# Cross-attention kernel: the second tile's scores moved from the second softmax phase to the main loop's begin, the third tile's into the second tile

## What is computed

```
hs     = mha(x @ Wq, enc @ Wk, enc @ Wv)            # 2048 queries x 150 keys, the main loop
ca_q1  = einsum('btc,th->bch', ca, Wq_ca)[:, idx]   # 384 different rows, spread over 2048
ca_hs1 = mha(ca_q1, x, x)                           # softmax over 2048: the two phases
ca_hs2 = mha(ca_hs1 @ Wq, ca @ Wk_ca, ca @ Wv_ca)   # 4 tokens: the small p
out    = (hs + ca_hs2) @ Wout + b_out + x
```

## Time and profile before

| | |
|---|---|
| median of 3 runs | 1533.33 us |
| the profiled execution, its own time | 1535.76 us |
| its span, first to last instruction | 1534.0 us |
| mean granted TensorE clock | 0.998 |
| TensorE matmuls busy | 98% of the span |
| VectorE, ScalarE busy | 51%, 41% |

### The profile page before, as it was taken

The page is one execution under the profiler, slowest core; times in us unless marked ns, Lnnn a source line. Parts: engine busy times, 40 slices in busy tenths (PEclk is TensorE's granted clock), DMA queues, the critical chain, the costliest instruction groups (busy, mean ns, idle before and its releaser), DMA issues.

```text
span 1534.0 us, 24564 instructions
## 1 busy us (share of the span) xinstructions
PE 1499.9 (98%) x10310; PEld 1246.0 (81%) x10310; DVE 789.5 (51%) x1596; ACT 622.5 (41%) x1311; POOL 2.8 (0%) x12
## 2 busy tenths in 40 slices
PE   7999999999999999999999999999999999999998
PEld 5764799999975489999987549999998745999998
DVE  6785435344478363444448726435345873453533
ACT  2438633333244852332332584323233377333322
POOL 0000000000000000000000000000000000000000
PEclk9999999999999999999999999999999999999999
DMA  6640011120252001140045100213004410021101
GB/s 237 225 156 1 7 57 66 57 110 27 104 192 95 1 20 52 57 157 18 27 149 176 57 1 20 90 37 148 9 35 165 172 37 2 19 95 57 61 18 44
DMA packets 46680, 117.28 MB, mean 76 GB/s; under 512 B 3661, under 2 KB 5317, under 8 KB 45019
## 3 DMA queue, kind: packets, MB, share of 16 engines
q1 hardware_dynamic: 37036, 93.91, 17.6%
q10 hardware_dynamic: 9535, 21.80, 3.7%
HBM read 77.33 MB, written 39.17 MB: 76 GB/s over the span
## 4 chain that ended last, share of the span: by engine, by line
PE 91%; DVE 4%; ACT 2%; issue 1%; DMA 1%; SPq 0%; ACTq 0%
PE ps_w L511 47%; PE ps_s L511 18%; PE ps_t L511 16%; PE ps_t L521 6%; PE ps_w L521 3%; DVE unit_max L1329 2%; ACT work L1133 1%; PE ps_s L521 1%; ACT ot L1047 0%; DMA xc<-in_L_xattn_Wv_ca_dram 0%; DMA xc<-in_x_dram 0%; DVE ca_mat L1345 0%; DVE ot L1441 0%; ACT ot L1116 0%; DVE xt_l L1355 0%
## 5 line engine op out<-in xcount | busy, mean ns | idle before, releaser
L511 PE MATMUL ps_w<-wo_h,ot 128*128 128x320 f32 x1280 | 310.4, 314 | 0.6 <-DVE ot L1441 0.6
L1329 DVE TENSOR_REDUCE unit_max<-ps_s 128x1 f32<-128x512 f32 x384 | 240.6, 683 | 54.6 <-PE ps_s L511 53.6
L1103 ACT ACTIVATE work<-ps_s,neg_max 128x150 f32<-128x150 f32 x512 | 152.1, 402 | 223.4 <-DVE neg_max L1387 223.4
L511 PEld LDWEIGHTS ps_w<-wo_h,ot 128*128 128x128 f32 x1280 | 220.2, 188 | 0.9 <-DVE ot L1441 0.9
L511 PE MATMUL ps_w<-wo_l,ot 128*128 128x320 f32 x640 | 197.4, 308 | 0.0
L511 PEld LDWEIGHTS ps_w<-v_all,work 120*128 120x128 f32 x1280 | 170.3, 190 | 3.1 <-issue 2.5
L511 PE MATMUL ps_w<-v_all,work 120*128 120x162 f32 (+1 forms) x1280 | 171.3, 288 | 0.0
L1383 DVE TENSOR_REDUCE neg_max<-ps_s 128x6 f32<-128x900 f32 x64 | 70.0, 1094 | 165.2 <-PE ps_s L511 165.2
L511 PE MATMUL ps_s<-keys_h,qt_h 128*128 128x300 f32 (+1 forms) x448 | 140.0, 312 | 0.0
L511 PE MATMUL ps_s<-keys_h,qt_l 128*128 128x300 f32 (+1 forms) x448 | 131.5, 293 | 0.0
L511 PE MATMUL ps_s<-keys_l,qt_h 128*128 128x300 f32 (+1 forms) x448 | 131.1, 293 | 0.0
(11 more groups left out here) (171 smaller groups left out, 2352.3 us busy)
## 6 DMA issues: line engine op xcount, KB each, us to landing
xc<-in_x_dram SPq DMA_DIRECT2D x32, 1280.0 KB, 6.4
out_dram<-work ACTq DMA_DIRECT2D x64, 320.0 KB, 2.2
xt_all<-work SPq DMA_DIRECT2D x60, 256.0 KB, 2.2
xt_l<-xt_all SPq DMA_DIRECT2D x12, 1280.0 KB, 5.6
y_all<-in_L_xattn_Wk_dram SPq DMA_DIRECT2D x4, 960.0 KB
y_all<-in_L_xattn_Wv_dram SPq DMA_DIRECT2D x4, 960.0 KB
pick<-pick_all SPq DMA_DIRECT2D x16, 194.0 KB
xc<-in_L_xattn_Wq_dram SPq DMA_DIRECT2D x1, 1600.0 KB, 10.7
```

What stands on the lines that cost most here:

```text
L511: return nc.tensor.matmul(out, lhs, rhs, start=start, stop=stop, skip_group_check=True)
L1103: return nc.scalar.activation(probs[:, h * KEYS:(h + 1) * KEYS], ps_s[:, bank, c * KEYS:(c + 1) * KEYS], exp, bias=neg_max[:, s % 2, h:h + ...
L1329: v.tensor_reduce(unit_max[:, a, n, q:q + 1], bank, AX_X, ALU.max).then_inc(max_free, 1)
```

## The change

`RUNS_IN` loses its entries for tile 1, so that phase 1 holds only tile 0's last runs. In the main loop TensorE computes `tile_scores(s + 1)` at every tile but the last, ahead of `values(s)`: tile 1's scores come in tile 0, and tile 2's come in tile 1, behind `project(0, 0)`. The split runs of tile 2 around `turn_o(0)` are gone. VectorE copies tile 0's turned weights ahead of the maximum of tile 1.

```diff
--- before.py
+++ after.py
@@ -155,8 +155,7 @@
 UNREAD = 4
 UNREAD_SUMS, UNREAD_SETUP = 3, 4
 ALL_RUNS = range(7)
-RUNS_IN = {(0, 14): ((0, 0),), (0, 15): ((0, 1),), (1, 0): ((0, 2),), (1, 1): ((0, 3),), (1, 2): ((0, 4),), (1, 3): ((0, 5), (0, 6)),
-           (1, 10): ((1, 0),), (1, 11): ((1, 1), (1, 2)), (1, 12): ((1, 3), (1, 4)), (1, 13): ((1, 5),), (1, 14): ((1, 6),)}
+RUNS_IN = {(0, 14): ((0, 0),), (0, 15): ((0, 1),), (1, 0): ((0, 2),), (1, 1): ((0, 3),), (1, 2): ((0, 4),), (1, 3): ((0, 5), (0, 6))}
 TURN_CA1, TURN_Z0, FIRST_EXP = 14, 8, 6
 
 
@@ -949,7 +948,7 @@
                         project(0, 0, range(0, 3))
                         gather(0)
                         project(0, 0, range(3, KT))
-                    elif 1 < s < SLOTS - 1:
+                    if s < SLOTS - 1:
                         tile_scores(s + 1)
                     elif s:
                         project(s - 1, 0)
@@ -958,9 +957,7 @@
                     values(s)
                     if s == 0:
                         turn_z(1)
-                        tile_scores(2, (0, 1))
                         turn_o(0)
-                        tile_scores(2, (2, 3, 4, 5, 6))
                     elif s < SLOTS - 2:
                         if s > 1:
                             project(s - 1, 0)
@@ -1452,8 +1449,8 @@
                     v.tensor_tensor(o_tile[:, s % 2, cols], out_banks[half], xc[:, c % 2 * ST + t, cols],
                                     ALU.add).then_inc((ya_ready, y_ready)[half], 1)
 
+                turned_weights(0)
                 maximum(1)
-                turned_weights(0)
 
                 shares = Steps(dve, dve_p2, b, 7)
                 by_head = lambda a: a[:, :, :].rearrange("p w (h t) -> p (w h) t", t=TOK)
```

## The result

The changed kernel takes 1547.62 us, the median of 4 runs (1546.88 to 1549.37); the kernel before 1532.88 in 4 runs on the same occasion. The ratio is 1.0093 (95% interval 1.0080 to 1.0105). The two medians are 14.7 us apart, which is 0.9% slower; against the 1533.33 us that the forecast started from it is 14.3. The profiled execution of the changed kernel took 1547.82 us, with a span of 1546.0.

The account below looks back on a forecast made before the run. TensorE, busy 98% of the span, and its waits for other engines were taken as the bound. Terms of -1.70 +2.84 -0.13 +0 -0.57 +2.84 make +3.28 us a batch, +13.1 on 1533.33: 1546.5 us, range 1542 to 1552.

Parts of the forecast that it names:

- (1): Second softmax phase: without tile 1's scores it ends 1.7 us earlier a batch, not 3.60, because ScalarE's queue holds it.
- (2): Ahead of tile 0's values: all 21 matmuls of tile 1's scores cover no wait and add 2.84 us a batch.
- (3): Values of tile 0: 0.13 us a batch less, as they no longer wait for VectorE's copy of the turned weights.
- (4): Values to tile 0's turned output: two runs of tile 2 leave, VectorE's chain keeps the 1.81 us; change 0.
- (5): Turned output to tile 1's values: five runs leave, -0.57 us to the gather; tile 2's scores behind the projection, +2.84 us.
- the first rival: Second phase not held by ScalarE: all 3.60 us of score stretches go, 1.4 us more a batch, 1539 us; chance 0.12.
- The clock: Rival: added waits in the phase and hand-over bring the clock down, 1557 us if once each batch; over 1552: chance 0.12.
- Only the matmul work counts: Rival for TensorE's whole work: denser matmuls and no idle time gain 4.5 us, 1529; faster 0.03, no change 0.03.

Follow-up runs that it names:

- the run with fewer exponentials: The changed kernel, leaving out five of the eight small exponentials of tile 0 in the second softmax phase: 1545.27 us, 1.0075 of the kernel before.
- VectorE's order alone: The kernel before with only VectorE's copy of tile 0's turned weights put ahead of the maximum of tile 1: 1533.90 us, ratio 1.0003.

## Why the prediction was right

The time, 1547.62 us against 1546.5, and the mechanism both held. Against the kernel before of the same occasion the change cost 14.7 us, where +13.1 was forecast; the difference of 1.6 us is nearly all in the stretch (+3.61 us a batch against +3.28). By its own steps, from the trace of batch 0:

| step | forecast | measured | from |
|---|---|---|---|
| (1) the phase ends earlier | -1.70 | -1.50 | 158.83 to 167.01, against 159.54 to 169.22 |
| (2) tile 1's scores | +2.84 | +2.87 | 169.00 to 171.87 |
| (3) values of tile 0 | -0.13 | -0.10 | 171.87 to 174.38 |
| (4) values to turned output | 0 | 0.00 | 174.38 to 176.19, 1.81 us as before |
| (5) up to the gather | -0.57 | -0.57 | 176.19 to 180.54, the forecast 4.35 |
| (5) rest of the projection | 0 | +0.04 | 180.54 to 182.01 |
| (5) tile 2's scores | +2.84 | +2.75 | 182.01 to 184.76 |
| tile 1's values and second half | 0 | +0.10 | 184.76 to 190.30, against 181.98 to 187.42 |
| sum | +3.28 | +3.59 | |

**(1) was the right account with one link missing.** From step 11 to step 14 ScalarE ran its small and large exponentials without a gap, 1.65 us a step, as forecast; the first exponential of step 14 came 4.95 us after that of step 11. But step 15 began 1.62 us after step 14 and not 1.40: its scores stand behind the summing of step 13 on TensorE, which had to wait for ScalarE's second half of that step. That is the loop over two steps of the run with fewer exponentials: from TensorE's `ps_t` half at 163.76 to ScalarE's 165.40 there are 1.64 us, and 1.69 there. ScalarE alone gives the pace only while it has a small exponential in each step, and even then by little. The forecast also took steps 7 to 9 before as dense, and expected steps 10 to 15 to be so; but TensorE turns the first phase's sums ahead of step 10's scores, and ScalarE idles before step 10, 0.34 us before the change and 0.35 us after it. It is the same in both, so it moves no term. That the phase is not held by ScalarE at all, the first rival, is out: 3.60 us of stretches went and 1.50 came back.

**(3) had the right size and a wrong reason.** The copy of the turned weights was never waited for, as VectorE's order alone shows. In the traces the values take 2.61 us behind the summing and 2.51 to 2.53 behind scores; the cause of that tenth was not tried. That the term came out at -0.10 is therefore luck. VectorE's maximum delays the first half of the normalisation by 0.24 us, contrary to the forecast, but not the second half, which the turned output waits for.

**(4) and (5) are shown** by trace and experiment. Two kernels that differ only in where tile 2's scores stand differ by 1.5 us a batch. The 1.81 us from the values to the turned output are the same in both kernels; what was hidden in them is paid for. The two waits are 1.19 and 0.85 us, somewhat under the 1.4 and 1.2 forecast, because the trace counts the tail of the preceding matmuls as busy; from start to start the distances are as worked out to 0.1 us (2.68 us from the turned output to the projection, against 2.73). One reading was wrong without moving the sum: between z_norm and the low half VectorE has six small operations, not ten.

**The clock** did not fall at the hand-over in the changed kernel's profiled execution: the stretches of all four batches are alike to 0.02 us. It falls elsewhere, in both kernels.

**Only the matmul work counts** is out with its sign. TensorE ran the same matmuls, 97% busy instead of 98%, and lost over 14 us: the second phase gave back 1.5 us a batch for work that costs 2.87 in a dense row.

## What to carry to other kernels

When matmuls move, ask at both ends what the engine does without them. A place where it waits for another engine is worth the wait's length, whatever the matmuls cost elsewhere; work taken from a place where two engines hand banks to each other in a loop comes back only until the other engine, or the loop itself, holds the pace: here 1.5 of 3.6 us. And measure a small gain on a stretch inside the trace that no clock fall touches: there 0.4 us in 182 could be read in every batch, where the medians of eleven runs could not tell it.

## What the runs showed of the hardware

The granted clock fell to the 1.2 GHz level at one place of the program, ahead of the softmax phases, in eight of the ten profiled executions, once or twice in each and in any of the four batches: 18 matmuls that take 3.39 us took 4.97 to 5.00 us, or 6.16 and 6.26 us. In the window from 842 to 849 of the earlier trace rows it was 0.51, and around the 18 slower matmuls of the changed kernel it was 0.69, a mean over a part at full clock and a part at the lower one (first the window ahead of them; length, then busy time of TensorE, its weight loads, VectorE, ScalarE and GpSimd, then the granted clock):

```profile
459.00:471.50 12.50, 12.06 (x77) 8.66 (x76) 10.39 (x18) 2.88 (x5) 0.00 (x0) 1.00 0.39 130
471.50:477.00 5.50, 5.50 (x25) 4.59 (x25) 2.95 (x7) 1.62 (x4) 0.00 (x0) 0.69 0.66 238
```

In the 12 to 13 us ahead of every one of these falls TensorE was 96% busy at a granted clock of 1.00; the clock did not fall at the 1.19 and 0.85 us of waiting behind tile 0, in any of the four batches of the changed kernel's trace. From stretch to stretch a fall costs 1.6 to 2.0 us, or 3.2 us where the 18 matmuls took over 6. The executions of the kernel before lie at 1532.1 to 1532.6 us where the mean clock is 1.000 and reach 1536.7 at 0.997, so most of that spread can be one, two or three such falls; this was not traced one by one.

Four groups of sums, each in its own 32 columns of the array, cost the same time as two: 0.78 and 0.77 us from the start of the summing to what follows.
